# Experts' stage with its loops written out and a re-ordered tail, and its normalisation moved into the attention before it

## The reference, cut to what matters

```
x = x + xattn1(layernorm(x))              # 16 heads of 16, causal, 256 keys from ctx_512
x = x + moe(layernorm(x))
layernorm(v) = (v - mean(v)) / sqrt(var(v) + 1e-5)
moe(xt):  p = softmax(xt @ Wg); e = argmax(p); gate = p[e]      # 8 experts
          each expert takes its first 256 tokens, in order of the tokens
          routed = gate * (silu(xd@W1[e]) * (xd@W3[e])) @ W2[e]  # back to its token, else 0
          shared = (silu(xt@sw1) * (xt@sw3)) @ sw2
          return routed + shared                                 # hidden width 352
```

## Time and profile before

| | |
|---|---|
| three runs | 1713.58, 1718.06, 1718.11 us (median 1718.06) |
| profiled execution | 1718.32 us, of which the span from first to last instruction is 1716.5 |
| busy: PE, DVE, ACT, POOL | 95%, 77%, 59%, 58% of the span |
| second attention, about | 1354 to 1534.5 us |
| experts' phase | 1534.5 to 1716.5 us |

### The profile page before, as it was taken

How to read it: one execution, slowest core, us unless ns; L and a number is a source line. 1 busy time by engine, 2 the same in 40 slices (tenths; PEclk the granted TensorE clock), 3 DMA queues, 4 the chain that set the end, 5 groups by cost and what they waited for, 6 DMA issues and landing times. The chain is left out here.

```text
span 1716.5 us, 49117 instructions
## 1 busy us (share of the span) xinstructions
PE 1632.6 (95%) x16165; PEld 1311.5 (76%) x16165; DVE 1320.2 (77%) x3025; ACT 1018.0 (59%) x2039; POOL 991.8 (58%) x879
## 2 busy tenths in 40 slices
PE   5889999999999999999999999999999899969898
PEld 4678888888888888888888888887886455548676
DVE  6888888888888888888888888887884588873123
ACT  5876666666666666666666666665333466642111
POOL 5348777878878787778788787777000222211221
PEclk8599999999999999999999999999999999987999
DMA  9721121121121122122112116114820000013244
GB/s 254 245 69 44 52 72 47 46 79 43 41 82 42 43 71 58 39 62 63 47 54 70 43 47 152 41 49 121 178 58 1 13 14 13 12 64 133 84 156 141
DMA packets 183005, 126.16 MB, mean 73 GB/s; under 512 B 107434, under 2 KB 170200, under 8 KB 182576
## 3 DMA queue, kind: packets, MB, share of 16 engines
q1 hardware_dynamic: 181424, 121.60, 25.7%
q0 software_dynamic: 1536, 3.99, 0.6%
HBM read 82.04 MB, written 24.48 MB: 62 GB/s over the span
## 5 line engine op out<-in xcount | busy, mean ns | idle before, releaser
L1174 POOL TENSOR_TENSOR c_rest<-c_prob 128x1024 f16<-128x1024 f32 (+1 forms) x513 | 796.0, 1572 | 242.8 <-ACT c_prob L963 232.5
L963 ACT ACTIVATE c_prob<-c_psS,ln,c_exp_scale 128x1024 f32<-128x1024 f32 (+1 forms) x514 | 536.5, 1044 | 241.2 <-PE c_psS L799 236.0
L1068 DVE TENSOR_REDUCE c_mxp<-c_psM 128x1 f32<-128x400 f32 (+1 forms) x1040 | 588.4, 572 | 113.8 <-PE c_psM L783 97.0
L799 PE MATMUL c_psS<-c_q,c_kk 128*128 128x256 f16 (+1 forms) x3350 | 512.7, 272 | 0.2 <-issue 0.2
L817 PE MATMUL c_psV<-c_vb,c_prob 128*128 128x129 f16 (+1 forms) x3328 | 396.5, 222 | 0.7 <-ACT c_acc L1017 0.7
L799 PEld LDWEIGHTS c_psS<-c_q,c_kk 128*128 128x128 f16 (+1 forms) x3350 | 321.8, 99 | 85.7 <-issue 0.4
L820 PE MATMUL c_psV<-c_vb,c_rest 128*128 128x65 f16 (+1 forms) x3328 | 374.2, 193 | 0.0
L783 PE MATMUL c_psM<-c_kkm,c_q 128*128 128x400 f16 (+1 forms) x1040 | 346.1, 333 | 4.7 <-DVE c_mxp L1068 3.0
L820 PEld LDWEIGHTS c_psV<-c_vb,c_rest 128*128 128x128 f16 (+1 forms) x3328 | 301.4, 99 | 22.1
L817 PEld LDWEIGHTS c_psV<-c_vb,c_prob 128*128 128x128 bf16 (+1 forms) x3328 | 305.3, 97 | 15.3 <-ACT c_acc L1017 1.0
L745 PE MATMUL c_psQ<-c_xb,c_w2s 128*128 128x256 f16 x1188 | 164.1, 275 | 5.8 <-PEq L162 4.0
(11 more groups left out here) (301 smaller groups left out, 2266.0 us busy)
## 6 DMA issues: line engine op xcount, KB each, us to landing
c_w2s<-w_scr SPq DMA_DIRECT2D x66, 256.0 KB, 2.6
c_ms<-m_scr SPq DMA_DIRECT2D x67, 192.0 KB, 2.3
c_w2s<-w_scr SPq DMA_DIRECT2D x66, 128.0 KB, 2.0
acc_scr<-c_acc SPq DMA_DIRECT2D x129, 64.0 KB, 2.0
kv<-acc_scr SPq DMA_DIRECT2D x16, 512.0 KB, 6.6
m_w<-in_L_ffn_W SPq DMA_DIRECT2D x16, 352.0 KB, 4.2
c_vb<-V SPq DMA_DIRECT2D x27, 129.0 KB, 2.0
c_kk<-KK SPq DMA_DIRECT2D x27, 128.0 KB, 2.0
```

The costliest lines, as they stand in the source:

```text
L799: mm = pe.matmul(psS[g % 2][0:r, i * S:(i + 1) * S], src[:, (lo + i) * P:(lo + i) * P + r], mov[slot][:, :], start=(one == 0 and i % 2 == ...
L963: nc.scalar.activation(prob[g][0:r, 0:w], psS[g % 2][0:r, 0:w], ACT.Exp, bias=keep["ln1024"][0:r, :], scale=exp_scale[slot][0:r, :]).then_ ...
L1068: nc.vector.tensor_reduce(mxp[:, st, c:c + 1], psM[:, st, 0:CHUNKS[c][1]], AX.X, ALU.max).then_inc(mx_done, 1)
L1174: nc.gpsimd.tensor_tensor(rest[g][0:r, 0:w], prob[g][0:r, 0:w], high[0:r, 0:w], ALU.subtract).then_inc(rest_done, 1)
```

## The change

1. `Norm` is gone from the experts' phase. In the second attention, in unit 4 of batches 1 to 7, DVE makes the statistics of the batch before (`statistics`), and a seed of the reciprocal root by integer arithmetic on the bits. After its own work of the batch, POOL refines this in three rounds of four small operations (`scale_of_rows`, every one waited for) and scales the two tiles (`rows_of`).
2. The last batch's statistics, seed, 12 small operations and scaling stand at the start of the experts' phase on DVE. PE starts its transposes there at once and waits for DVE before the eighth group only.
3. The loops of both phases on PE, ACT and DVE are written out, and those of the attention on SP and POOL; SP's loop that loads the experts' weights stays.
4. Tail: two quarters of the routed rows are added between the last `gated` operations, the other two before the last `add_shared`, and `x` is stored in six pieces, the last two of one tile each.

```
@@ phase_attention1, DVE, in batch(b), unit k
+                    if k == 4 and not first:
+                        statistics(b - 1)      # 2 bn_stats, 2 bn_aggr, 3 tensor_scalar
@@ phase_attention1, POOL
+            def batch(b, u, first=False):
+                pool.wait_ge(s_full, UNITS * b + 1)
+                mask_keys(nc, ahead, kT, nxt(b), 1 - u)
+                pool.wait_ge(pv_done, UNITS * b + 2)
+                place_values(nc, ahead, v, nxt(b), 1 - u)
+                if not first:
+                    rows_of(b - 1)             # waits for `seeded`
@@ helper of both
+def scale_of_rows(compute, last, tiles, link):
+    y, half, tmp = last["rstd"][:, tiles], last["half"][:, tiles], last["tmp"][:, tiles]
+    for _ in range(ROUNDS):                    # ROUNDS = 3
+        link(compute.tensor_tensor(tmp, y, y, ALU.mult))
+        link(compute.tensor_tensor(tmp, tmp, half, ALU.mult))
+        link(compute.tensor_scalar(tmp, tmp, -1.0, 1.5, ALU.mult, ALU.add))
+        link(compute.tensor_tensor(y, y, tmp, ALU.mult))
@@ phase_moe, PE
-            norm.tensor(pe)
-            norm.wait_columns(pe)
+            for k in range(NT // 2):
+                if k >= len(psH):
+                    pe.wait_ge(turned_out, k + 1 - len(psH))
+                if k == NT // 2 - 1:
+                    pe.wait_ge(rows_done, ST)
...
-            with pe.Fori(1, HEAD // 2) as j:
-                for u in range(2):
-                    n = 2 * j + u
-                    shared(n, n, (n - 1, sw2, 1 - u))
+            for n in range(2, HEAD):
+                shared(n, n, (n - 1, sw2, 1 - n % 2))
@@ phase_moe, SP
+            for lo, hi in ((0, 4), (4, 8), (8, 12), (12, 14), (14, 15), (15, 16)):
+                sp.wait_ge(x_final, min(lo // 4 + 1, 4))
+                if lo >= NT - 2:
+                    sp.wait_ge(y_done, 2 * TAILS[-1][0] + 3 + lo - (NT - 2))
```

More of the change, by code:

```diff
@@ L15 @@
 U32 = mybir.dt.uint32
+I32 = mybir.dt.int32
 AX = mybir.AxisListType
@@ L2032, in _ @@
             batch(0, 0, first=True)
-            with pe.Fori(0, B // 2 - 1) as j:
-                batch(2 * j + 1, 1)
-                batch(2 * j + 2, 0)
+            for b in range(1, B - 1):
+                batch(b, b % 2)
             batch(B - 1, 1)
@@ L2077, in _ @@
             batch(0, first=True)
-            with act.Fori(0, B // 2 - 1) as j:
-                batch(2 * j + 1)
-                batch(2 * j + 2)
+            for b in range(1, B - 1):
+                batch(b)
             batch(B - 1)
@@ L2144, in _ @@
             batch(0, 0, first=True)
-            with dve.Fori(0, B // 2 - 1) as j:
-                batch(2 * j + 1, 1)
-                batch(2 * j + 2, 0)
+            for b in range(1, B - 1):
+                batch(b, b % 2)
             batch(B - 1, 1)
@@ L2156, with phase_moe @@
 FT1 = [(0, 128), (128, 128), (256, 96)]
-def phase_moe(nc, ctx, t, keep, x, rows, xT):
+def phase_moe(nc, ctx, t, keep, last, x, rows, xT):
     def sb(name, shape, dt=F32):
@@ L2412, in own @@
                 silu(HEAD + e, u)
[L2414 to L2415 removed]
+            for k in range(NT // 2):
+                act.wait_ge(turned, k + 1)
+                nc.scalar.activation(xT[:, :, 256 * k:256 * (k + 1)],
+                                     psH[k % len(psH)][:].rearrange("p (c s) -> p c s", c=DK),
+                                     ACT.Copy).then_inc(turned_out, 1)
             act.wait_ge(l_done, 2)
             nc.scalar.activation(ex[:], ex[:], ACT.Exp).then_inc(ex_ready, 1)
[L2418 to L2420 removed]
+            for n in range(HEAD):
+                silu(n, n % 2)
             act.sem_inc(xt_done, 1)
[L2422 to L2424 removed]
+            for e in range(E1):
+                own(e, e % 2)
             for n, _ in TAILS:
@@ L2501, in _ @@
             nc.vector.tensor_copy(s_idx[:], slot[:]).then_inc(idx_ready, 1)
[L2502 to L2507, removed]
+            for n in range(2, HEAD):
+                gated(n, n % 2, (0,))
+                add_shared(n - 1, n - 1)
+                gated(n, n % 2, (1, 2))
             add_shared(HEAD - 1, HEAD - 1)
@@ L2636, in build @@
         rows = sb(whole, "xn_rows", [P, NT, RW])
+        last = {
+            "stats": sb(whole, "l_stats", [P, NT, 6]),
+            "agg": sb(whole, "l_agg", [P, NT, 2]),
+            "rstd": sb(whole, "l_rstd", [P, NT]),
+            "half": sb(whole, "l_half", [P, NT]),
+            "tmp": sb(whole, "l_tmp", [P, NT]),
+        }
         xn = rows[:, :, 0:D]
```

127 lines of the change are left out of this document (92 added, 35 removed).

## The result

| | before | after |
|---|---|---|
| median | 1718.07 us (five runs, 1713.58 to 1718.16) | 1704.9 us (four runs, 1702.00 to 1707.27) |
| profiled execution, its span | 1718.32, 1716.5 | 1705.68, 1703.9 |

A fifth run of the changed kernel took 2208.48 us at a mean clock of 0.70 and is left out. The ratio of the times is 0.9928, 95% interval [0.9908, 0.9947]: faster, by more than the 0.3% that can be told. The forecast of 1700.8 us, range 1695 to 1713, holds it, but one step of it failed: the pause of 9.45 us did not go, and one of 5.1 us is left. That is as much as the profiled execution's distance from the forecast, 1705.7 against 1700.8, since the errors of the other terms, 0.3 to 0.8 us each, nearly cancel.

A forecast was written before the change was run, and what follows sets the result against it. PE, busy 95% of the span, was taken as the bound, with DVE in the attention. From 1718.3 us, -9.3 + 0.8 + 4.9 - 1.7 - 9.45 - 2.8 gave 1700.8 us, range 1695 to 1713.

The forecast's parts named there:

- the pause of 9.45 us: Shared stages of the experts' phase: late products at PE's loop branch, taken as gone once loops are written out; -9.45 us.
- Normalisation: Start of the experts' phase: router starts near 1541.7 because DVE's short chain and PE's transposes run side by side; -9.3 us.
- Clock behind the router: Router and shared stages: the half-clock phase may fall better or worse, up to twice as long; mean +0.8 us.
- Statistics in the attention: Unit 4 of seven batches: DVE's seven added instructions, 1.6 us, partly covered, cost 0.7 us a batch; +4.9 us.
- the faster copy to `g_recx`: Attention, unit 5: DVE's copy no longer slowed by POOL's `mask_keys` beside it, giving back 0.45 us.
- Loops in the attention: Attention: written-out loops save 0.29 us in each of six batches, as already-written-out batch 7 suggested; -1.7 us.
- Rival 1: Shared stages: the pause is tied to POOL's scatter, not the branch, and stays; 1710.2 us, chance 0.27 if kept whole.
- half of the pause staying: Shared stages: half the pause remains, as one faster run suggested; 1705.5 us, chance 0.13.
- the whole pause: Shared stages: the pause stays at full length beside POOL's scatter; 1710.2 us, chance 0.27.
- Tail: End of the program: routed quarters fit DVE's idle times and stores go out earlier; -2.8 us.
- Rival 3: PE's written-out code: code blocks arriving late make new pauses; 1729.1 us with two more and the old kept, chance 0.05.

The follow-up runs named there:

- e4: Changed kernel with POOL's scatter held back some 8 us, until DVE has added stage 2 to x; 1709.38 us, ratio 0.9959 to the kernel before.
- e10: Kernel before the change, with POOL waiting after its first 8 scatters until they have landed; 1707.98 us, ratio 0.9998 to the kernel before.
- e11: Changed kernel with its 16 scatters broken by one wait into 12 and 4; 1700.27 us, ratio 0.9961 to the kernel before.
- e12: Changed kernel with the scatter in two halves of 8 and the old end of the program; 1703.99 us, ratio 0.9976 to the kernel before.
- e3: Changed kernel without DVE's statistics and POOL's refining and row scaling in the attention; 1701.00 us, ratio 0.9915 to the kernel before.
- e8: Changed kernel with DVE's attention statistics spread over units 1 and 2 (batch 6's stay) and the seed on POOL; 1704.51 us, ratio 0.9909 to the kernel before.
- e1: Changed kernel without POOL's 16 scatters, the experts working on empty rows; 1699.48 us, ratio 0.9900 to the kernel before.
- e5: Changed kernel with POOL waiting after its first 8 scatters until they have landed; 1700.59 us, ratio 0.9892 to the kernel before.
- e2: Changed kernel with the hardware loops put back in the experts' phase on PE, DVE and ACT; 1706.59 us, ratio 0.9940 to the kernel before.
- e9: Changed kernel with the scatter in two halves, statistics spread over units 1 and 2, and seed on POOL; 1697.35 us, ratio 0.9935 to the kernel before.

## Why the prediction was right, and where it was not

*Normalisation* (-9.3 forecast, -9.6 measured): right, and DVE's path ended last, as said. PE needs 3.25 us for its 28 transposes, 0.12 each and not the 0.22 that I took from the earlier trace rows (the granted clock was 1.00 here, and 0.50 there until 1548), and then waits 2.29 us for DVE's rows. DVE's chain took 5.4 us, one operation of it 0.49 instead of 0.18.

*Clock behind the router* (+0.8): 0.0 this time. The experiments show a wider spread than my "up to twice 3.3": 19.1 us in three profiles, 20.7 in seven, 22.05 in one, 23.5 to 23.7 in three. Two executions of one program may differ by it, so it belongs in the range and not in the sum. Nor is a short router all gain: in the three profiles with 19.1 us (e4, e10, e11), and in e12, the granted clock had been 0.50 once already, from 1533 or 1534 on, and the last batch's addition came 1.1 to 1.4 us later for it (17.57, 17.51 and 17.83 us instead of 16.39 after the one before, 17.01 instead of 15.64 in e10).

*Statistics in the attention* (+4.9): +4.5, the size right. 0.62 a batch against 0.7, with 1.64 us inserted. So 1.0 us was covered, about as much as I had, but not all by what I had named. I had said that nothing comes back a unit later, where PE waited for DVE already; but just that wait, 0.44 us before and 0.33 in e3, is gone in the changed kernel, and so are 0.38 and 0.37 us that DVE idles in e3 before unit 4's drain and unit 5's maxima. Whether the faster copy to `g_recx` gave back the 0.45 us that I gave it is not shown: e3 and e8 have slow copies at 21.09 and 21.08 us, where they cost nothing, but e3's DVE idles 0.39 us soon after, and the changed kernel's only 0.16; no run has slow copies and the statistics in unit 4 together. The Trainium skill's rule (GPSIMD Engine Reference, § Specifications), by which POOL's two tiles would have lengthened that copy, had its condition unmet: POOL's small operations stand beside the copy, which took 0.29, and its tiles come later:

```profile
1444.64 0.20 POOL L1866 TENSOR_TENSOR l_tmp<-l_rstd 128x2 f32<-128x2 f32 x1
...
1445.81 2.43 POOL L1962 TENSOR_SCALAR xn_rows<-x_rows,l_agg,l_rstd 128x256 f32<-128x256 f32 x2
1448.20 3.75 POOL L1845 TENSOR_TENSOR km<-kT,g_hmask 128x1024 f32<-128x1024 f32 x2
```

*Loops in the attention* (-1.7): -1.3. Batch 7's 21.06 in the earlier trace rows was the right measure; five batches had it to gain and not six.

*The pause* (-9.45, measured -4.4): this is the step that failed. I tied it to PE's loop branch because it began there. The branch is gone and the pause is there; e1, e4 and e5 show that it belongs to POOL's 16 scatters in a row. Its beginning at the branch was a coincidence of place: 9 to 11 us into the scatter fall within the stage behind it. The 4.4 us that did go may be the loops' share (e2), which I had as the whole; so that the measured time still lies in the range is in part luck. Rival 1 had the cause, with half of the pause staying at 1705.5 us, against 1705.68 measured; I gave that 0.13, and the whole pause 0.27. That its number fits so well is luck too, since the half was a guess from one faster run. The argument that I set against it, that the written-out stages 6 and 7 have none, was worthless, as no scatter of 16 runs beside them. The Trainium skill's rule on taken branches (Runtime: NRT & Kernel Launch, § Instruction fetch mechanics) would have had the whole pause gone with the branch; here 5.1 us stayed without any branch, and PE's own products ran without a gap while the signals were late.

*Tail* (-2.8): -2.4, its own by e12. DVE ends 3.3 us after the last `down` starts, as forecast; the last store lands 3.4 us after that and not 2.5.

*Rival 3*, code arriving late: refuted, there is no new pause on PE in the attention, twice the code though it is (additions 21.70 to 21.72 us apart in every batch up to the last).

What is open: why PE's signals are late from 8 to 10 us into a run of indirect DMAs; whether it is their number or the unbroken time; by what way the loops add to it; and why one chip of three shows no lateness at all.

## What to carry to other kernels

A pause that begins at a branch is not a pause by the branch: look at what every other engine has been doing for the last 10 us, and move that. Sixteen indirect DMAs in a row beside matmuls whose signals are waited for deserve a wait in the middle; it cost 2.5 us of POOL's time and took away a pause of 5 us (e5), and cost nothing on a chip that shows no such pause (e10). When a profile and a time come from different chips, look first whether both chips show the effect. Work put into a full engine's program is free in the units where it idles, and costs 0.6 us where another engine waits for the next instruction; what fits into the cover stays cheap even there. In unit 4 of the last batch four operations (1.0 us) cost 0.11 us, and all seven (1.64 us) 0.75.

## What the runs showed that I had not expected

- During a run of indirect DMAs of POOL, semaphores that PE's products set reached ACT up to 7.2 us late, some 5 us apart (1587.30, 1592.30, 1597.27), and DVE up to 8.7 us late (e4), while PE's products themselves ran at full pace and DVE's and ACT's signals, as far as the rows show, came in time. The profiles with eight or more in a row showed it in the first two series and not on the chip of the third (e9 to e12).
- The same kernel took 1707.8 us on one chip and 1717 to 1719.5 on two others, a difference almost as large as the change's gain; the mean granted clock was 0.974 there and 0.972 on the other two.
- The half-clock stretch behind the router was 13.7 us long before and in the changed kernel and 20.5 in e9, with PE busy for 19.81 of these.
- On POOL the small 128x2 operations took 0.20 us each and followed one another every 0.28 us with a wait behind each, against 0.17 and 0.20 on DVE.
